# Indirect gathers of embedding rows: many in flight, or one at a time

## What is computed

```python
e = stack([tbl_f[ids[:, f]] for f in range(26)], axis=1)      # 512 x 26 x 64, float32
x = layer_norm(dense @ Wd.T, gd, bd)                          # 512 x 128
y = layer_norm(einsum('bnd,ed->bne', e, Ws), gs, bs)          # 512 x 26 x 128
y = layer_norm(einsum('bne,pn->bep', y, Wsi), gsi, bsi)       # 512 x 128 x 32
T = concatenate([x[:, None, :], swapaxes(y, 1, 2)], axis=1)   # 512 x 33 x 128
Z = einsum('bnd,bmd->bnm', T, T)[:, TRIL_I, TRIL_J]           # 512 x 528
z = (layer_norm(Z @ Wl.T, gl, bl) * mask)                     # the first 384 columns are kept
h = relu(concatenate([z, dense], 1) @ W_top1 + b_top1)
h = relu(h @ W_top2 + b_top2)
out = h @ W_top3                                              # 512 x 1
```

## Time and profile before

| | us |
|---|---|
| median of 2 timed runs | 196.54 |
| lowest and highest | 195.52, 197.56 |
| span of the profiled execution | 318.9 |
| mean granted TensorE clock in it | 0.775 of full speed |

### The profile page before, as it was taken

The page is one execution under the profiler, slowest core; times in us unless marked ns, Lnnn a source line. Parts: engine busy times, 40 slices in busy tenths (PEclk is TensorE's granted clock), DMA queues, the critical chain, the costliest instruction groups (busy, mean ns, idle before and its releaser), DMA issues.

```text
span 318.9 us, 4779 instructions
## 1 busy us (share of the span) xinstructions
PE 184.9 (58%) x1794; PEld 132.2 (41%) x1794; DVE 119.3 (37%) x356; ACT 111.7 (35%) x478; POOL 101.2 (32%) x118
## 2 busy tenths in 40 slices
PE   0566340001111100000799999999999989998976
PEld 0444220001010000000566776567875678756756
DVE  3542210210000000000484888575576655776520
ACT  1133110100000000000745887376674667744332
POOL 4787777777777777710000000000000000000000
PEclk9956575555555555555579999999999999999998
DMA  4841111111111111100000011001200002010000
GB/s 162 271 166 25 27 32 25 25 29 25 28 26 25 29 25 25 28 8 0 0 2 0 2 40 31 1 2 23 45 3 2 2 20 44 8 22 14 2 0 0
DMA packets 14861, 9.91 MB, mean 31 GB/s; under 512 B 12099, under 2 KB 12501, under 8 KB 14582
## 3 DMA queue, kind: packets, MB, share of 16 engines
q1 hardware_dynamic: 11078, 5.22, 6.0%
q0 software_dynamic: 3328, 3.41, 5.6%
q10 hardware_dynamic: 432, 0.97, 0.9%
HBM read 7.76 MB, written 0.00 MB: 24 GB/s over the span
## 4 chain that ended last, share of the span: by engine, by line
PE 41%; another core or an unknown queue 35%; ACT 9%; DVE 6%; issue 3%; DMA 2%; POOL 2%
PE py L387 10%; PE tu L371 5%; PE pf L437 5%; PE pz L402 4%; PE pf L418 4%; ACT junk L576 2%; PE py L384 2%; ACT ysq L584 2%; PE tu L365 2%; PE pf L447 2%; DVE proj L811 2%; POOL emb L337 2%; ACT u_sd L580 1%; ACT zT L615 1%
## 5 line engine op out<-in xcount | busy, mean ns | idle before, releaser
L337 POOL DMA_INDIRECT emb<-tables_dram,rows_at x104 | 99.0, 952 | 31.6 <-issue 31.4
L818 DVE TENSOR_REDUCE y_ms<-ysq 128x16 f32<-128x512 f32 x32 | 21.9, 684 | 134.3 <-ACT ysq L584 117.2
L371 PE MATMUL tu<-proj_w,embT 128*128 128x256 f32 x104 | 36.4, 433 | 60.5 <-ACT embT L570 43.1
L387 PE MATMUL py<-wbd,proj 128*128 128x192 f32 (+4 forms) x256 | 58.3, 339 | 22.4 <-issue 22.4
L387 PEld LDWEIGHTS py<-wbd,proj 128*128 128x128 f32 x256 | 44.0, 212 | 36.1 <-issue 35.2
L371 PEld LDWEIGHTS tu<-proj_w,embT 128*128 128x128 f32 x104 | 19.3, 212 | 65.0 <-ACT embT L570 44.1
L594 ACT ACTIVATE gram<-pz 64x272 f32<-64x272 f32 x32 | 12.1, 379 | 85.8 <-remote 85.6
L402 PE MATMUL pz<-T 128*32 128x34 f32 x1024 | 25.8, 200 | 27.8 <-issue 26.1
L402 PEld LDWEIGHTS pz<-T 128*32 128x32 f32 x1024 | 21.1, 114 | 39.7 <-issue 37.1
L576 ACT ACTIVATE junk<-tu 128x128 f32<-128x128 f32 x104 | 27.4, 272 | 22.3 <-remote 12.4
L811 DVE SCALAR_TENSOR_TENSOR proj<-tu,u_r,comb_w 128x128 f32<-128x128 f32 x104 | 31.7, 347 | 1.8
(11 more groups left out here) (127 smaller groups left out, 174.0 us busy)
## 6 DMA issues: line engine op xcount, KB each, us to landing
emb<-tables_dram,rows_at POOLq DMA_INDIRECT x104
w<-w_dram SPq DMA_DIRECT2D x1, 1280.0 KB
wl<-wl_dram SPq DMA_DIRECT2D x1, 1024.0 KB
zn<-gram SPq DMA_DIRECT2D x24, 32.0 KB, 1.9
zr<-gram SPq DMA_DIRECT2D x24, 32.0 KB, 1.9
denseT<-denseT_dram ACTq DMA_DIRECT2D x1, 512.0 KB
w<-w_dram SPq DMA_DIRECT2D x1, 512.0 KB
comb_w<-comb_w_dram ACTq DMA_DIRECT2D x1, 311.0 KB, 3.2
```

The source lines that it names most:

```text
L337: pool.indirect_dma_start(emb[:, k, :], None, t["tables"], bass.IndirectOffsetOnAxis(ap=rows_at[:, k // HALF, k % HALF:k % HALF + 1], axis=0),
L371: pe.matmul(TU[(PAIRS * g + j) % NTU][:, P:P + 2 * E], embT[:, j, :], proj_w[:, P:], start=True, stop=True).then_inc(u_done, 1)
L387: mm = pe.matmul(PY[(QUARTERS * g + q) % NPY][:, :, :].rearrange("p b c -> p (b c)")[:, col:col + n], proj[:, j, tile % 2, :], wbd[:, :, : ...
L818: dve.tensor_reduce(y_ms[:, q, :], ysq[:, q % 2, :, :], AX_X, ALU.add).then_inc(y_ms_ready, 1)
```

## The change

Ahead of each gather but the first, GpSimd waits until the gather before it has landed. `(k - 1) // 2` is that gather's pair; the threshold is 16 if it is the first of its pair and 32 if it is the second.

```diff
             def gather(tiles):
 
                 for k in tiles:
+                    if k:
+                        pool.wait_ge(gathered[(k - 1) // 2], 16 + 16 * ((k - 1) % 2))
                     pool.indirect_dma_start(
                         emb[:, k, :], None, t["tables"],
                         bass.IndirectOffsetOnAxis(ap=rows_at[:, k // HALF, k % HALF:k % HALF + 1], axis=0),
```

## The result

| | us |
|---|---|
| before, median of 2 runs | 196.54 (195.52 to 197.56) |
| after, median of 2 runs | 340.61 (340.46 to 340.75) |
| ratio | 1.738, 95% interval 1.726 to 1.750 |
| span of the profiled execution after | 338.9 |

The changed kernel takes 1.74 times as long. The forecast was 322 us, with 291 to 345 us as its range.

A forecast was written before the change was run, and what follows sets the result against it. The prediction took TensorE to bound the undisturbed kernel, and the gathers' round trip the changed one. First issue 4.9, gathers 269.9, load phase 5, last landing 2.4 and tail 40.7 sum to 322.9, stated as 322 us, range 291 to 345.

The forecast's parts named there:

- load phase: From 9.6 to 19.2 us, with the DMA engines full, about two gathers land later: +5 us, bounds +3 to +8.
- tail: Work left after the last pair lands, steps 48 to 51 and last layers: 40.7 us, bounds 39 to 46.
- The cadence is the round trip: On GpSimd's queue, each gather takes a full round trip, 2.62 us (2.35 to 2.75), instead of 1.25 us; 80 in 100.
- waking counted twice: In the gather cadence, a tenth below 2.72 us, since GpSimd's waking may already be in the waiter's 2.42 us.
- TensorE would wait over 2 us in each step: At line 362, two gathers take 5.24 us a step against 2.85 us of work, up to step 48.
- Memsets behind the waits: GpSimd's memsets of lines 347 to 354 run at about 42 us instead of 21.7 us, at no cost.
- The later weight loads: SyncE's twelve weight loads are released about 1.4 us later, hidden because they are wanted only at step 6.
- The stall: 112.9 us on "another core or an unknown queue", mostly between 40 and 151 us, taken as only the profiled execution's.
- Hidden wait: Rival: gathers far enough ahead of use that GpSimd's waits change nothing, 196.5 us; 3 in 100.
- Shorter round trip: Rival: without the profiler a gather's landing costs less, cadence 2.1 to 2.3 us, about 277 us; 8 in 100.
- Dearer restart: Rival: GpSimd's issue costs more after a wait than back to back, cadence 3.0 us, 362 us; 6 in 100.
- VectorE in GpSimd's way: Rival: gathers beside a busy VectorE each take 0.6 us more, 385 us; 2 in 100.

The follow-up runs named there:

- late_loads: Kernel before, no added gather waits, with SyncE's twelve weight loads waiting for pair 3 instead of pair 0: 196.8 us, ratio 0.9995, chip B.
- change_again: The changed kernel run once more, unaltered, on chip C: 345.8 us, ratio 1.084 to the kernel before there.
- two_in_flight: The change, but each gather waits for the gather two before it: 309.0 us, ratio 0.974 to the kernel before, chip A.
- paced: The change with each landing wait replaced by a GpSimd scratch fill of 1320 floats: 303.5 us, ratio 0.960 to the kernel before, chip A.
- wait_even: The change with the wait ahead of every second gather only: 262.8 us, ratio 0.832 to the kernel before, chip A.
- paced_mid: The change with each landing wait replaced by a GpSimd scratch fill of 510 floats: 234.0 us, ratio 0.735 to the kernel before, chip C.
- paced_short: The change with each landing wait replaced by a GpSimd scratch fill of 210 floats: 248.0 us, ratio 0.778 to the kernel before, chip C.
- three_in_flight: The change, but each gather waits for the gather three before it: 317.3 us, ratio 1.003 to the kernel before, chip A.
- pe_fetch: The change with 32 long-met waits added in each of TensorE's 52 steps: 349.0 us on chip C.
- more_fetch: The change with 3 x 1024 long-met waits added on SyncE's queue ahead of the stacking of groups 0 to 2: 345.2 us on chip B.

## Why the prediction was right, and where it was off

The span of the change and the sum, term by term (us):

| term | predicted | measured |
|---|---|---|
| first issue | 4.9 | 4.85 |
| 103 quiet periods | 269.9 (2.62 each) | 279.2 (2.711 each) |
| load phase | +5 | +5.6 |
| landings late beside an instruction fetch | not in the sum | +8.2 |
| all other excess | not in the sum | +0.6 |
| landing of the last | 2.4 | 2.5 |
| tail | 40.7 | 37.95 |
| median less the profiled span | not in the sum | +1.7 |
| sum | 322.9 | 340.6 |

**The cadence is the round trip.** Right, and it is the step that decides. The case had 80 in 100; the time lies at 340.6 in its 291 to 345. One waiter's row told it: 2.42 us from issue to the next instruction, and 0.30 us gap, 2.72 together. The term that was mis-sized is the 0.10 us which I took off again, for a "waking counted twice"; it is most of the gap between 2.62 and 2.711. The trace has 2.45 + 0.26 = 2.71: nothing was counted twice. 103 times over it is 9 us, half of the miss. That TensorE would wait over 2 us in each step was a little high: between 24 and 150 us it is busy 84.7 us in some 23 steps, 3.7 us a step at clock 0.57 and not 2.85, and waits about 1.8.

**Late landings.** The sum gave 5 us for the load phase, where it measured 5.6, and nothing for the 100 other gathers. In the trace of before GpSimd waits for no landing, so such lateness didn't add up. This term of 8.2 us is the other half of the miss. In a chain of waits the mean counts, not the median.

**The tail.** 40.7 predicted, 37.95 measured, 39.0 in `late_loads`. 37.95 us is below the lower bound of 39 that I gave this term. The low clock that I allowed 5 us for didn't come in this execution (1.00 from 301 us on), but it did on chip C: 0.60 in the first 10 us of `change_again`'s tail, which took 41.8 us. So the right clock here was chance, and the bound of 46 had its reason.

**Memsets behind the waits.** They were said to cost nothing. They begin when the issue of gather 12 is through and end at 46.1 us, at about its landing; gather 13 is issued only 0.73 us later, at 46.84. That period is 3.16 us: 0.45 us over, once. The later weight loads cost nothing that can be seen.

**The stall.** The step "I take the stall for a part of the profiled execution alone" was wrong. The kernel before takes 314.6 to 320.0 us in timed runs on two of the three chips named. The sum didn't rest on it, since its terms are taken outside the stall and the changed kernel has none. But what the change is worth does: 1.74 times the time on one kind of chip, 1.08 times on the other. And the sign of a gentler change depends on it: half of the waits is 0.83 on A, where the sum for a chip like B says 1.3.

**The rivals.** Hidden wait: TensorE waits at nearly each pair, and twelve waits at the start alone cost 22 us; out. Shorter round trip: no landing is under 2.3 us, out; the Trainium skill's estimate ("DMA: Bandwidth & Descriptors", section "Anatomy of one DMA — SWDGE (gpsimd) path"), 2.08 us and 298 us by its cadence, is 0.4 us a gather under the measured 2.45 us. Dearer restart: the issue is 942 ns after a wait as without, and the gap even shorter, 0.26 us; out. VectorE in GpSimd's way: gathers are busy 99.5 us in all, against 99.0 before, although VectorE works beside all of them now; out.

**What stays open.** What the stall is. Its mark is that TensorE and ScalarE hold instructions whose data is there, while GpSimd issues on at its own pace; in `two_in_flight` GpSimd itself waits for the landings and still issues every 1.36 us, so they do arrive, and TensorE stands still all the same. The stalled traces also hold fewer semaphore updates (2,431 in that of before, 2,702 and 2,809 with three and two in flight, against 4,034 of the change and 3,770 of `late_loads`). Most of what is missing is landings of gathers. Each gather should leave 16 such records. There are 16 a gather in both traces of the change and in `paced`, 12 in `wait_even` and in `paced_mid`, 6.6 in `paced_short`, and 4.3, 3.5 and 2.2 in `two_in_flight`, `three_in_flight` and before; on chip B, `late_loads` keeps 15.6 at 1.28 us a gather. So on A and C more records are missing the closer the gathers come, and some are missing before a stall shows. That could mean that the writing of the records is what holds the engines up on these chips. Every later execution was recorded, so this can't be told from a stall of the kernel's own, and wasn't tried. It also makes the shares of "another core or an unknown queue" rough, since releasers are inferred from these events; the times don't depend on it. The threshold between 1.54 and 1.79 us is from one kernel on either side. Whether a block fetch delays a gather through a shared DMA engine is inferred from the overlap and its shift, and wasn't shown engine by engine.

## To carry to other kernels

Serialising small indirect DMAs replaces the issue interval by the full round trip: here 2.71 for 1.25 us at 32 KB. Compare it with what the consumer needs per transfer (here 1.42 us); two in flight would be about enough (median 1.36 us, but mean 1.43 on chip A with its late landings), three would be (mean 1.31). Neither was run on a chip without the stall. In a chain of waits, add every disturbance that the old pipeline hid, by its mean over the whole chain. And where the profiled span and the timed runs differ by more than a few per cent, don't explain it away: time the kernel on several chips before a change is judged by a ratio.

## What the runs showed of the hardware that was not expected

- The same program took 197.0 us on one chip and 316.6 and 317.5 us on two others, each within 2% over 7 to 23 runs, all recorded.
- On those two the traces lose landing records of gathers: 16 a gather are left at 2.46 us a gather and above, 12 at 2.04 and 1.79, 6.6 at 1.54, under 5 below; on the first chip 15.6 are left at 1.28 us.
- On those two, spacing the gathers further apart makes the kernel faster: on C 317.5 us (1.27 us a gather in the trace of before), 248.0 at 1.54, 234.0 at 1.79, and slower again beyond (345.8 at 2.86); on A 316.6 us, 262.8 at 2.04, 303.5 at 2.46.
- A 16 KB block of TensorE's instructions, about 1 us on the DMA engines, goes with a delay of a 32 KB gather whose data moves at the same time: 0.5 to 1.1 us in the first trace of the change, up to 1.3 in `change_again` and 1.5 in `pe_fetch` and `more_fetch`, and at the same nine gathers in both traces of the change.
- After a stretch in which TensorE waits for gathers, the same tail took 37.9 us where the clock was at its higher level from its start, and 41.8 us where it was at 0.60 in its first 10 us.
